# Edge stage of a graph attention kernel: node maxima and scales for eight node tiles at once, and bf16 parts summed on TensorE

## The reference, cut to what matters

```python
h = (xn @ W).reshape(N, HEADS, HEAD_DIM)                # 8 heads of 32
a_src = jnp.einsum('nhd,hd->nh', h, att_src)
a_dst = jnp.einsum('nhd,hd->nh', h, att_dst)
e = jax.nn.leaky_relu(a_src[src] + a_dst[dst], NEG_SLOPE)
emax = jax.ops.segment_max(e, dst, num_segments=N)
ee = jnp.exp(e - emax[dst])
denom = jax.ops.segment_sum(ee, dst, num_segments=N)
alpha = ee / denom[dst]
agg = jax.ops.segment_sum(h[src] * alpha[:, :, None], dst, num_segments=N)
```

## Time and profile before

| | us |
|---|---|
| median of 3 runs | 2312.43 (2310.39 to 2313.22) |
| the profiled execution | 2315.37 |
| its span, first to last instruction | 2314.1 |

### The profile page before, as it was taken

One profiled execution on the slowest core, in us unless ns is written; L12 is line 12 of the kernel. 1 busy time (PEld: TensorE's weight loads), 2 busy tenths in 40 slices (PEclk: granted clock), 3 DMA queues, 4 the chain that ended last, 5 costly groups with the idle time before them and its releaser, 6 DMA issues.

```text
span 2314.1 us, 40198 instructions
## 1 busy us (share of the span) xinstructions
PE 1761.5 (76%) x11202; PEld 1505.1 (65%) x11202; DVE 1801.5 (78%) x5534; ACT 1553.3 (67%) x3225; POOL 1185.9 (51%) x1167
## 2 busy tenths in 40 slices
PE   6626666666666666666656799999399999999998
PEld 4514445544445544455544688898399999999997
DVE  7449999999999999999999788887455555555554
ACT  3367667776667766667763687787367777776665
POOL 3277777777777777777770124444322222222223
PEclk9857777777777777777777899999699999999999
DMA  7767766777766677766773223322735346435432
GB/s 230 190 192 214 214 204 201 206 212 214 213 201 204 206 211 212 211 194 202 208 209 123 64 79 98 101 88 73 241 61 120 48 108 161 100 48 155 85 48 37
DMA packets 283217, 357.89 MB, mean 155 GB/s; under 512 B 118629, under 2 KB 227006, under 8 KB 280562
## 3 DMA queue, kind: packets, MB, share of 16 engines
q1 hardware_dynamic: 218578, 202.63, 28.5%
q0 software_dynamic: 63840, 151.61, 26.4%
q10 hardware_dynamic: 576, 1.09, 0.2%
HBM read 464.93 MB, written 95.79 MB: 242 GB/s over the span
## 4 chain that ended last, share of the span: by engine, by line
PE 58%; DVE 26%; issue 8%; ACT 2%; POOL 2%; DMA 2%; DVEq 1%; SPq 0%; ACTq 0%; POOLq 0%
PE bank L962 16%; PE bank L1169 8%; PE bank L1157 8%; PE bank L1158 7%; PE bank L1159 7%; PE bank L1168 4%; DVE edge_mem L1031 3%; DVE win_mem L1056 3%; PE bank L840 2%; DVE edge_sum L1075 2%; DVE piece_lo L1153 2%; DVE seg_max L1067 1%; POOL edge_mem L774 1%; PE bank L949 1%; PE bank L841 1%
## 5 line engine op out<-in xcount | busy, mean ns | idle before, releaser
L774 POOL DMA_INDIRECT edge_mem<-node_table,src_col x880 | 842.1, 957 | 283.1 <-issue 256.7
L962 PE MATMUL bank<-edge_mem 128*128 128x264 f32 x1760 | 526.8, 461 | 7.4 <-ACT edge_mem L903 4.3
L962 PEld LDWEIGHTS bank<-edge_mem 128*128 128x128 f32 x1760 | 385.5, 226 | 105.6 <-issue 24.1
L1899 POOL DMA_INDIRECT out<-expert_mem,slot_tok x112 | 174.5, 1558 | 489.6 <-DVE expert_mem L1836 469.5
L1886 ACT ACTIVATE expert_mem<-bank,par 128x256 f32<-128x256 f32 x448 | 224.7, 502 | 187.0 <-PE bank L1159 186.9
L1153 DVE TENSOR_TENSOR expert_rounded<-expert_mem,expert_rounded 128x512 fp32r<-128x512 f32 x280 | 193.5, 691 | 196.7 <-ACT expert_rounded L1886 123.4
L1031 DVE TENSOR_TENSOR edge_mem<-edge_mem,bank 128x1056 f32<-128x1056 f32 x385 | 294.1, 776 | 13.9 <-ACT bank L895 13.9
L1169 PE MATMUL bank<-expert_rounded 128*128 128x512 f32 x784 | 278.8, 395 | 0.0
L1157 PE MATMUL bank<-expert_rounded 128*128 128x256 f32 x896 | 255.0, 285 | 27.4 <-DVE expert_rounded L1153 27.4
L868 ACT ACTIVATE edge_mem<-iota,dst_col 128x128 bf16<-128x128 bf16 x880 | 262.8, 387 | 0.0
L1158 PE MATMUL bank<-expert_rounded 128*128 128x256 f32 x896 | 254.8, 284 | 0.0
(11 more groups left out here) (245 smaller groups left out, 4202.8 us busy)
## 6 DMA issues: line engine op xcount, KB each, us to landing
expert_rounded<-split_w SPq DMA_DIRECT2D x114, 2048.0 KB
edge_mem<-step_place SPq DMA_DIRECT2D x55, 512.0 KB, 7.0
split_w<-piece_hi SPq DMA_DIRECT2D x72, 256.0 KB
split_w<-piece_lo SPq DMA_DIRECT2D x72, 256.0 KB
piece_full<-in_L_ffn_W SPq DMA_DIRECT2D x64, 256.0 KB
expert_mem<-expert_rows SPq DMA_DIRECT2D x224, 64.0 KB, 2.9
edge_mem<-node_table,src_col POOLq DMA_INDIRECT x880
node_table<-win_mem SPq DMA_DIRECT2D x12, 544.0 KB, 4.9
```

The costliest lines, as they stand in the source:

```text
L774: pool.indirect_dma_start(gath[g % NGB][:, t, :], None, node_table, bass.IndirectOffsetOnAxis(ap=src_col[:, k, t % 2:t % 2 + 1], axis=0)). ...
L962: ins = pe.matmul(bank[4 + at % 3][:, 0:AGG], onehot[g % 2][:, 2 * k + j, :], gath[g % NGB][:, 2 * k + j, 0:AGG], start=(j == 0), stop=(j ...
```

## The change

- `node_chain`: the first instruction that reads the node maxima takes them from PSUM, already summed. Instead of eight copies (L991) between eight maxima (L994), two copies take the old maxima and `a_dst` of all eight consecutive windows at once; the eight maxima into the windows follow, each still waiting for the one before; then new and old scores of the eight *windows* (not steps) are made.
- The scales are those of windows: one multiplication of eight windows, 128x2112 (new L1035), replaces eight of 128x264 (L1052). It stands after the first of the four small message pieces, and the adds (L1060) wait for it and, as before, for each other.
- PE adds the bf16 parts in PSUM: three matmuls of 16 columns (new L932) for each edge tile where one of 48 stood, and three of 9 columns (new L951) where one of 27 stood. The reductions L981 and L1075 go; scores and mask read PSUM.
- Since node values now stand by window and an edge tile needs that of its step, PE reads the group's word (new L909) and takes the address of the 48 matmuls of L932 from registers.
- The word gets a three-bit difference for all eight steps; it is made in fewer, wider instructions, once, in the setup, and POOL makes one more small constant there. ACT's exponential waits for the scale instead of the last add.

```diff
-                for k in range(1, GS):
-                    t = step(dve.tensor_single_scalar(win_delta[:, :, k], win_delta[:, :, k], 3 + 3 * k, ALU.logical_shift_left))
...
+                t = step(dve.tensor_tensor(win_delta[:, :, :], win_delta[:, :, :], win_shift[:, :, :], ALU.logical_shift_left))
...
-                        act.wait_ge(added, GS * g)
+                        act.wait_ge(scaled, g)
...
+                if 0 <= g < NG:
+                    word = pe.value_load(win_word[0:1, g:g + 1], min_val=0, max_val=(1 << 30) - 1)
...
                     for t in range(GT):
-                        ins = pe.matmul(edge_bank(t), onehot_t[g % 2][:, t, :], parts[:, t // 2, :, :].rearrange("p i c -> p (i c)"),
-                                        start=True, stop=True)
+                        if t % 2 == 0:
+                            j = nc.s_assert_within((word >> (6 + 3 * (t // 2))) & 7, 0, GS - 1,
+                                                   skip_runtime_bounds_check_because="three bits of the word")
+                        for i in range(3):
+                            ins = pe.matmul(b_edge[:, t, :], onehot_t[g % 2][:, t, :], parts[:, bass.ds(j, 1), i, :].rearrange("p o c -> p (o c)"),
+                                            start=(i == 0), stop=(i == 2))
...
-                            ins = pe.matmul(b_ms[:, k * MW:(k + 1) * MW], o16[:, 2 * k + j, :],
-                                            cand[:, j, k, :, :].rearrange("p i c -> p (i c)"), start=(j == 0), stop=(j == 1))
+                            for i in range(3):
+                                ins = pe.matmul(b_ms[:, k, :], o16[:, 2 * k + j, :], cand[:, j, k, i, :],
+                                                start=(j == 0 and i == 0), stop=(j == 1 and i == 2))
...
-                dve.tensor_reduce(ms, b_ms.rearrange("p (k i c) -> p k c i", i=3, c=HEADS + 1), AX.X, ALU.add).then_inc(maxima_read, 1)
...
+                step(dve.tensor_copy(nodeval[:, :, 0:HEADS], win[:, ws, ROW:WROW]))
+                t = step(dve.tensor_copy(old[:, :, :], win[:, ws, AGG:ROW]))
+                yield
                 for k in range(GS):
                     w = window(g, k)
-                    if k:
-                        dve.wait_ge(dve_step, t)
-                    t = step(dve.tensor_copy(old[:, k, :], win[:, w, AGG:WROW]))
-                    yield
                     dve.wait_ge(dve_step, t)
                     t = step(dve.tensor_tensor(win[:, w, AGG:ROW], win[:, w, AGG:ROW], newm[:, k, :], ALU.max))
                     yield
...
+            def scale_windows(g):
+                acc = win[:, windows(g), 0:AGG].rearrange("p w (h c) -> p w h c", c=HC)
+                if g >= 1:
+                    dve.wait_ge(added, GS * g)
+                dve.wait_ge(weights_ready, g + 1)
+                dve.tensor_tensor(acc, acc, scale.unsqueeze(3).to_broadcast([P, GS, HEADS, HC]), ALU.mult).then_inc(scaled, 1)
...
+                        if k == 0:
+                            scale_windows(p)
...
-                    for b, o_, first_, end in edge_banks:
-                        t = step(dve.tensor_reduce(ev[:, first_:end, :], b[:, o_:o_ + (end - first_) * EW].rearrange(
-                            "p (t i c) -> p t c i", i=3, c=2 * HEADS), AX.X, ALU.add))
...
-                    t = step(dve.tensor_tensor(score[:, :, :], gb[:, :, AGG:ROW], ev[:, :, 0:HEADS], ALU.add))
+                    t = step(dve.tensor_tensor(score[:, :, :], gb[:, :, AGG:ROW], b_edge[:, :, 0:HEADS], ALU.add))
```

More of the change, by code:

```diff
@@ L150, in build @@
         win_row = sb1("win_row", [1, NSTEP], I32)
-        win_delta = sb1("win_delta", [1, NG, GS], I32)
+        win_delta, win_shift = (sb1(n, [1, NG, GS], I32) for n in ("win_delta", "win_shift"))
         win_word = sb1("win_word", [1, NG], I32)
@@ L330, in build @@
         edge_vals, scored, weights_ready, weighted = sem("edge_vals"), sem("scored"), sem("weights_ready"), sem("weighted")
-        summed, added = sem("summed"), sem("added")
+        summed, scaled, added = sem("summed"), sem("scaled"), sem("added")
         edge_setup = sem("edge_setup")
@@ L677, in build @@
         b_asrc, b_cand = bank[0], bank[0]
[L678 to L687, removed]
+        b_edge = bank[1][:, 0:GT * 2 * HEADS].rearrange("p (t c) -> p t c", c=2 * HEADS)
+        b_ms = bank[7][:, 0:GS * (HEADS + 1)].rearrange("p (k c) -> p k c", c=HEADS + 1)
         b_exp = bank[2][:, 0:(GT + GS) * HEADS].rearrange("p (t h) -> p t h", h=HEADS)
@@ L996, in node_chain @@
                 dve.wait_ge(dve_step, t)
-                if g >= 1:
-                    dve.wait_ge(edge_vals, g)
-                step(dve.tensor_tensor(newm[:, :, :], newm[:, :, :], old[:, :, 0:HEADS], ALU.max))
-                t = step(dve.tensor_copy(nodeval[:, :, 0:HEADS], old[:, :, HEADS:2 * HEADS]))
-                yield
-                dve.wait_ge(dve_step, t)
-                for m in (newm[:, :, :], old[:, :, 0:HEADS]):
-                    t = step(dve.tensor_tensor(m, m, nodeval[:, :, 0:HEADS], ALU.add))
+                step(dve.tensor_tensor(newm[:, :, :], win[:, ws, AGG:ROW], nodeval[:, :, 0:HEADS], ALU.add))
+                t = step(dve.tensor_tensor(old[:, :, :], old[:, :, :], nodeval[:, :, 0:HEADS], ALU.add))
                 yield
@@ L1046, in edges_dve @@
                             next(small, None)
+                        if k == 0:
+                            scale_windows(p)
                         w = window(p, k)
                         acc = win[:, w, 0:AGG]
-                        acc_h = acc.rearrange("p (h c) -> p h c", c=HC)
+                        next(small, None)
+                        dve.wait_ge(scaled, p + 1)
                         if at:
                             dve.wait_ge(added, at)
-                        t_scaled = step(dve.tensor_tensor(acc_h, acc_h, scale[:, k, :].unsqueeze(2).to_broadcast([P, HEADS, HC]), ALU.mult))
-                        next(small, None)
-                        dve.wait_ge(dve_step, t_scaled)
                         dve.wait_ge(summed, at + 1)
```

46 lines of the change are left out of this document (25 added, 21 removed).

## The result

The changed kernel takes **2327.06 us** (median of 5 runs, 2324.97 to 2327.93) where the kernel before takes 2312.43 (2310.39 to 2313.79): 1.0064 times as long, 95% interval 1.0051 to 1.0077. It is slower, as forecast, but by 14.6 us and not by 40.

A forecast was written before the change was run, and what follows sets the result against it. DVE was taken to bound the kernel, gathers and the loop through PE close behind. New period 15.5 + E (5.6) = 21.1 us against 20.4; 54 periods give 38 us, the last group +1: 2352 us, range 2290 to 2430.

The forecast's parts named there:

- What bounds the kernel before: Edge stage: DVE is the busiest engine, 20.23 us a group, with POOL's gathers (20.2) and a DVE-PE circle close behind.
- the loop through PE: PE waits for DVE's parts (2.64 us) and split (3.39 us) in every group, so work added there may not be free.
- Period of before: Time from one group's node chain to the next in the kernel before, taken as 20.4 us.
- DVE's part by part: DVE's instructions a group: reductions 1.04 us gone, wide scale saves 0.5, scores to next chain 5.10; busy 2.2 to 3 less.
- Where the parts come ready: DVE's new order walked from the node chain's first instruction: the last part ends at 10.1 us, where it was 12.5.
- The stream E: PE after the wait for the parts: 40 register instructions (3.7 us) and 48 register-addressed matmuls (1.9), E = 5.6 us.
- The rival to which I gave 0.07: An even match on PE: matmuls at 0.026, register instructions at 0.093, E = 4.95, period 20.5, 2316 us; chance 0.07.
- The break-even: Length of PE's edge stream at which the new period equals the old 20.4 us: E = 4.9.
- The rule on matmuls: PE's edge matmuls at the skill page's 62 ns for microcode decoding: E would be 6.7, time about 2412 us.
- The rule on clocks: PE's sequencer at 1.2 GHz against DVE's 0.96: register instructions 3.0 us instead of 3.7, period 20.4, time unchanged.
- The rival of the gathers: POOL's gathers become the bound if E is under 4.65: period 20.2, 2296 us; chance 0.33, including cases that gain less.
- What would show it: Signs: period 21.1, 48 matmuls over 5 to 6 us, DVE idle 2 to 3 before scores, POOL waiting some 40 more.

The follow-up runs named there:

- Moving the product away: Kernel before with 14 of 16 gathers, residual product on PE moved from behind the second sum to behind the sixth: 2296.74 us.
- early-read kernel: Changed kernel with the word loaded and 16 of 40 register instructions moved after the fourth sum, ahead of the wait for the parts: 2299.14 us.
- both experiments that shortened E: Changed kernel with fixed addresses for the 48 edge matmuls, 2297.51 us, and with the word and 16 register instructions moved earlier, 2299.14 us.
- in the old order with the product moved: Kernel before with both sums of bf16 parts on TensorE, all sixteen gathers, residual product behind the sixth sum: 2297.52 us.
- both sums in the old order: Kernel before with edge values and node maxima both summed from bf16 parts on TensorE, nothing else of the change: 2307.18 us.

## Why the prediction was right or wrong

- **What bounds the kernel before**: DVE, with the gathers and the loop through PE close behind. Right: with 14 gathers it took 2312.57, no less than with sixteen. What I missed in the same trace is the second place where the loop closes, at the third add, 0.27 us in the group that I read and 13.7 us over 40 groups. I had passed over it as no gap over 0.3. Moving the product away was worth 16 to 17 us where the gathers left room.
- **Period of before**, 20.4: too low by 0.12, the mean over all groups was 20.52 and stood in the earlier trace rows. 54 x 0.12 = 6 us of the error.
- **DVE's part by part**: right. Forecast 2.2 to 3 us less in a group, measured 2.5; wide scale 2.3 to 2.4, measured 2.35; from scores to the next chain 5.10, measured 5.08.
- **Where the parts come ready**: 10.1 forecast, 10.51 measured, 0.41 too early (22 us). Up to the end of the third add the walk was exact (7.4, measured 728.19 - 720.75 = 7.44). The four small instructions and the fourth add, which I had ended at 9.0, ended at 730.10 - 720.75 = 9.35: the add starts 0.20 late behind its register instructions, and the small ones took 0.15 longer in all. The rest is 0.06.
- **The stream E: the step that failed, a term that was mis-sized.** 5.6 forecast, 4.85 measured in the forecast's terms, 0.75 too much (40 us). It was a sum of 3.7 for 40 register instructions and 1.9 for 48 matmuls. The first was nearly right: 40 x 0.097 = 3.9. The second was twice too much: of the 4.95 between the records 1.07 are left for the matmuls, 0.17 of it the last one's own length, so 0.019 each; the early-read kernel's 3.42 - 24 x 0.097 leaves 1.09. "Half as much again, 0.04, since their address has to be filled in" had no row behind it: a matmul whose address comes from a register is issued no slower than a fixed one. The rival to which I gave 0.07 had the stream right: matmuls at 0.026 and register instructions at 0.093, E = 4.95. Its time, 2316, was low by the parts' 0.41, less the period's 0.12 and the 0.10 by which the stream's two ends were shorter than the 0.33 put for them.
- **Altogether**: 0.7 forecast, less 0.75, plus 0.41, less 0.12, and 0.04 in small terms: 0.28 a group, 15 us. The break-even by the measured terms is E = 20.52 - 15.92 = 4.6. The kernel was 0.25 us on the wrong side of it.
- **The direction was in part luck.** With E at 4.85 and all else as forecast, the period would have been 15.5 + 4.85 = 20.4, that of before, and the forecast "no change". It came out slower because the parts were late as well: two errors of 0.75 and 0.41 with opposite signs, each larger than the 0.28 that was to be forecast.
- **The rule on matmuls** of the Trainium skill, "TensorE: Matmul & The Clock Gate", section "Wait — 56ns, not 53.3ns?": 62 ns for a matmul decoded by microcode. The traces don't show a register address taking that way: in the early-read kernel 48 such matmuls took 2.44 us with most of 24 register instructions among them, and 48 x 0.062 alone would be 3.0, an estimate from that page.
- **The rule on clocks** of the Trainium skill, "Advanced Engine Details and Errata", section "Clock Domains": by it a register instruction would have cost PE 0.074, an estimate from that page. The ratio of clocks doesn't carry over in these traces: it cost PE 0.097. On DVE the register instructions of L991 start 0.077 to 0.080 us apart in the records of the kernel before; the forecast's 0.093 was a remainder and had something else in it. By the rule the forecast would have been no change.
- **The rival of the gathers** (2296 if E is under 4.65) held in both experiments that shortened E, 2297.5 and 2299.1; in the old order with the product moved the gathers bind as well, 2297.5.
- **What would show it**: DVE idle before the first score with PE's edge matmuls as releaser, 1.64 and not 2 to 3 us; 48 matmuls over 4.00, or 4.95 with what stands ahead, and not 5 to 6; POOL waited for PE 24.6 + 7.2 us where it was 15.9, not 40 more.

## What to carry to other kernels

Work that is cheap in the sum of an engine can be dear in a place: 40 instructions that no busy time counts, all behind the wait of a loop through two engines, took back all 2.5 us a group of DVE's work and more. Put register work ahead of the wait where what it reads is known earlier: sixteen instructions moved there made the stream 1.6 us shorter and the kernel faster than the one before. When an engine has been relieved and the time doesn't move, look for the next place where the same two engines wait for each other, and for work in front of it that nobody there needs; a floor such as the gathers' has to be lowered first for that to be seen.

## What the runs showed of the hardware

- Register instructions on PE's queue start 0.097 us apart, or 0.124 with a matmul between, and show 0.036 or 0.046 us in the record. On DVE's queue those of L991 start 0.077 to 0.080 apart. In none of the views' busy times do they count.
- A matmul with its address in a register needs no more issue time than one with a fixed address (0.02 to 0.03 us). Its cost is the register instructions ahead of it.
- The wait for the parts stands on the first register instruction of the stream, and the whole stream follows it: its first record starts 0.21 us (mean) after the parts end, in the changed and in the early-read kernel. The early-read kernel's 24 register instructions and 48 matmuls took 3.42 us, where 24 x 0.097 + 48 x 0.02 = 3.3.
- The first eight records of sums in a group run at a granted clock of 0.50, its level of 1.2 GHz, behind a stretch in which PE waited for the split: 3.89 before, 3.86 in the changed kernel, 3.87 with both sums in the old order. In the last two, forty-eight matmuls of 9 columns stand just ahead of them, and the granted clock was 0.50 all the same.
